# Row maxima that go to the shift row by DMA alone, tokens in another order, and new places in the plan

## The chip, the cores and the metric

The kernel runs on one core of a Trainium2 chip. Its time is that of one execution on the device, in microseconds (us); before and after are given as medians of several runs.

## The reference

Four transformer blocks run one after the other on x of shape (4, 512, 256), four batch entries of 512 tokens with 256 features; everything is float32. Each block has its own conditioning from `cond` (4, 256). Block 0 has one attention head over all 256 features; blocks 1 to 3 have 16 heads of 16 features. Cut to what the change touches, blocks 2 and 3 are:

```python
# block 2
h = layernorm(x, g1, be1) * (1 + scale_msa) + shift_msa
attn = softmax(einsum('blhd,bmhd->bhlm', q, k) * HD ** -0.5)      # q, k, v from h, 16 heads
x = x + gate_msa * (einsum('bhlm,bmhd->blhd', attn, v) @ Wproj + bproj)
x = x + gate_mlp * mlp(layernorm(x, g2, be2) * (1 + scale_mlp) + shift_mlp)
# block 3
att = softmax(einsum('bhqd,bhkd->bhqk', q, k)) / D ** 0.5
h1 = out_projection(att @ v) + x
x = h1 + sln(h1)
```

Block 1 normalises q and k to unit length (cosine attention) and has gates and an MLP like block 2. A softmax over the keys needs, for each query and head, something near the largest score to subtract before the exponential.

## The kernel before

**Jobs and layers.** The program works on 16 jobs, job j being layer j // 4 (the four blocks) for batch entry j % 4. Layers 1 to 3 are the many-headed ones (`multi(j)`); layer 1 is `bounded(j)`: there a cheap bound takes the place of the true maximum ("gmax", "shift1", "crow"). Layers 2 and 3 compute true maxima. A job's 16 heads are 4 units of 4 heads; units are numbered through, 4 j + g. All of this is unrolled, and nothing is looped on the chip.

**The plan.** `plan_steps` writes out one order of steps (kind, job or unit, index), from tables that give for each kind of step a time in ticks relative to its job: `QKV`, `ATTN`, `FFN`, `FFN3`, `OUTPUT`, `LAST`, `FOR_LAYER`, `FOR_LAST`, `SINGLE0` to `SINGLE3`, and so on. A job has 16 ticks (`TICKS`), 4 for a unit. Every engine walks through that one order and emits what it has to do for each step, so a place in a table sets the place in each engine's instruction stream. `PAIR`, `PAIR1`, `PAIR7` and `PAIR_LAST` say for every two ticks how scores, maxima, the products with V ("av") and the other steps ("0", "1") are mixed. `START` is the order of the first steps, given by hand.

**Attention of a unit.** SyncE stacks parts of q and k of the unit's heads into `SQ[u % 4]` and `SK[u % 4]` ("stack", six DMAs of 128 KB): rows 0 to 62 hold one head, rows 64 to 126 another, for two halves. Rows 63 and 127 of `SQ` are the shift row: minus the maximum of each query, which meets a 1 in `SK`, so the product that gives the scores already has the shift in it.

1. "max", 16 steps per unit, six ticks (`LEAD`) ahead of the unit's scores: a matmul (L657) of 128 queries (stationary, from `SQ`) against all 512 keys into a PSUM bank, and on VectorE a reduction (L1179) that writes minus the maximum of the 128 queries, one per partition, into a column of `m16`.
2. "shift", once per unit, four ticks after the unit's first maxima: TensorE waits for the last two maxima and transposes 80 columns of `m16` into a bank (L672); VectorE copies 16 rows of it into `cT` (L1186); SyncE waits for the copy and sends them with two DMAs (L554), 8 rows of 512 bytes each, to rows 63 and 127 of `SQ`.
3. "scores", 16 steps: a matmul (L680) of 128 keys against 512 queries, whose first waits for that transfer (`shifted`), and an exponential on ScalarE (L871) into one of 12 buffers `probs`.
4. "av": four matmuls (L693) on four column strips of the array, then a copy of the bank `AVB` to `oU`.

A maximum matmul takes rows 0 to 62 or 64 to 126, and the scores matmul beside it the other half, so the two run in pairs.

**Banks.** Everything but "av" uses seven PSUM banks in turn (`RING`): `claim` waits until the step seven uses earlier has been read out.

**Tokens.** "hT1" transposes the normalised input of a job from `tok1` (tokens on partitions, four tiles of 128) into a bank (L626) with token 128 t + p in column 128 t + p. At a job's end "oT1" transposes `oU` back (L718), from columns 128 i to 128 i + 127 to tile i. SyncE's queue is one queue for stacks, shift rows, weight loads, gates and stores, in the order of the plan.

The scratch of the step "headscale" (once, early) is in `m16`.

Of the kernel before, what the change touches and what calls it, by code (L numbers as in the profile page):

```python
# [13 lines left out]
P = 128  # L14
# [41 lines left out]
def direct(j):  # L56
# [5 lines left out]
SINGLE0 = {"stat1": (-16.0,), "norm1": (-19.05,), "hT1": (-15.0, -14.24), "q": (-9.06, -5.21), "k": (-5.7, -4.45),  # L62
           "v": (3.06, 6.72), "scores0": (-0.45, -0.1, 1.86, 3.41), "soft0": (1.86, 2.41, 4.61, 5.17),
           "pT0": (6.87, 7.42, 7.68, 8.53), "av0": (10.18, 10.73), "proj": (12.39, 13.94), "stat2": (13.99,),
           "norm2": (14.84,), "bias": (-2.75,)}
SINGLE1 = {"stat1": (-20.05,), "norm1": (-12.3,), "hT1": (-11.18, -11.13), "q": (-8.12, -4.91), "k": (-8.57, -5.36),
           "v": (3.1, 4.42), "scores0": (-1.64, -1.29, 1.78, 1.88), "soft0": (2.49, 2.84, 3.36, 3.71),
           "pT0": (7.11, 7.47, 7.82, 8.68), "av0": (11.73, 12.09), "proj": (13.16, 13.51), "stat2": (13.82,),
           "norm2": (14.33,), "bias": (-3.4,)}
SINGLE2 = {"stat1": (-17.0,), "norm1": (-16.55,), "hT1": (-9.6, -9.29), "q": (-6.76, -3.56), "k": (-5.65, -3.7),  # L70
           "v": (3.0, 4.07), "scores0": (-0.14, 0.81, 1.88, 2.23), "soft0": (2.59, 3.44, 3.96, 4.51),
           "pT0": (7.92, 8.38, 8.63, 8.99), "av0": (12.74, 12.9), "proj": (14.18, 14.28), "stat2": (16.29,),
           "norm2": (16.84,), "bias": (0.5,)}
FFN0 = {"hT2": (16.72, 17.27), "fc1": (20.62, 20.98, 21.33, 21.74, 24.73, 25.09, 26.87, 27.22), "gelu": (22.09, 27.58),
        "fc2a": (25.06, 25.81), "fc2": (30.32, 32.88)}
FFN2 = {"hT2": (24.65, 24.83), "fc1": (25.13, 25.31, 25.49, 25.67, 30.12, 30.29, 31.19, 31.87), "gelu": (26.05, 31.95),
        "fc2a": (28.47, 29.21), "fc2": (32.16, 32.27)}
FIRST = {("v", 0, 0): -4.01, ("v", 0, 1): -2.2, ("modrow", 0, 1): 1.96, ("headscale", 1, 0): -0.04, ("mod", 0, 1): 3.47,
# [3 lines left out]
NEXT1 = {("modrow", 1, 0): 16.25, ("mod", 1, 0): 22.0, ("load_mod", 1, 1): 24.0, ("modrow", 1, 1): 30.8,  # L82
         ("mod", 1, 1): 31.5, ("load_gate", 1, 0): 35.3, ("split_qkv", 1, 0): 45.87, ("load_qkv", 1, 1): 42.17,
         ("split_qkv", 1, 1): 49.41, ("load_qkv", 1, 2): 48.44, ("split_qkv", 1, 2): 49.75, ("load_qkv", 1, 0): 42.0,
         ("vones", 4, 0): 56.19, ("vones", 5, 0): 67.95}
LEAD_IN = {"stat1": (-25.59,), "norm1": (-23.73,), "hT1": (-14.74, -14.56), "qktok": (-12.53, -12.04, -11.51, -10.77),
           "qkss": (-12.22, -11.69, -11.15, -10.61), "qkroot": (-10.43,), "v": (-7.19, -6.91), "qkrs": (-10.19,),
# [3 lines left out]
           "shift1": (-0.98,), "crow": (-0.9, -0.22, 1.7, 1.7)}  # L91
# [118 lines left out]
def plan_steps():  # L210
# [4 lines left out]
    for w in range(BATCH, JOBS):  # L215
# [71 lines left out]
def cond_blocks_kernel(nc, x, cond, cols, rows, wqkv, wp, w1, w2, wmod, wgate, out):  # L287
# [3 lines left out]
    with ExitStack() as ctx:  # L291
# [1147 lines left out]
```

## Time and profile before

| | |
|---|---|
| median of 3 runs | 1176.04 us (1174.32 to 1178.96) |
| the profiled execution's own time | 1179.31 us |
| its span, first to last instruction | 1177.5 us |
| granted TensorE clock, mean | 0.98 |
| busy: TensorE, ScalarE, VectorE, GpSimdE | 94%, 69%, 60%, 42% |
| transfers on the hardware queue | 36288 packets, 63.20 MB, 20.1% of 16 engines' span |

The engines are PE (TensorE matmuls), PEld (its weight loads, which overlap them), DVE (VectorE), ACT (ScalarE), POOL (GpSimdE) and SP (SyncE, which issues the DMAs). "L672" is a line of the kernel's file. The busy time of an instruction includes its latency, and matmuls overlap, so the busy share of PE is above what the array is really in use. The name `m` in the rows is the tile `m16`, and `tok` stands for both `tok1` and `tok2`.

### The profile page before, as it was taken

The page shows a single profiled execution, that of the slowest core. Times are in us where ns is not written, and L with a number is a line of the kernel's source. Part 1 is how long each engine was busy: PE and PEld are TensorE (multiplying, and loading weights), DVE is VectorE, ACT ScalarE, POOL GpSimd, SP SyncE. Part 2 cuts the span into 40 slices and gives each one's busy share as a digit, 9 for nine tenths or more (in the row PEclk, how much of TensorE's full clock was granted, in tenths as well). Part 3 has the DMA queues.
Part 4 walks back from the last instruction along what each step waited for, and adds up shares of the span by engine and source line. Part 5 has one row for each costly group of instructions (what it writes and reads, how often), then busy time and mean ns, then how long its engine had stood idle before and what let it go on. Part 6 is the DMA issues. An engine that isn't in the chain of part 4 may idle for free.

```text
span 1177.5 us, 19700 instructions
## 1 busy us (share of the span) xinstructions
PE 1106.8 (94%) x6681; PEld 708.5 (60%) x6681; DVE 705.0 (60%) x1448; ACT 807.3 (69%) x1439; POOL 491.3 (42%) x447
## 2 busy tenths in 40 slices
PE   7799999889999999999999999999999999999985
PEld 5476877655665656657656566556566566545443
DVE  6463538535165364235864855865855756888884
ACT  2563655478788778796686776687686676676763
POOL 2452642523633635453345453354253345243232
PEclk8899999999999999999999989999999999999998
DMA  7010000223212203320122231132022202232201
GB/s 230 9 37 2 27 10 10 62 57 100 81 34 74 72 1 82 82 63 12 44 74 81 60 82 32 24 82 63 24 60 55 53 12 77 55 81 54 83 2 46
DMA packets 36386, 64.45 MB, mean 55 GB/s; under 512 B 7208, under 2 KB 22312, under 8 KB 36288
## 3 DMA queue, kind: packets, MB, share of 16 engines
q1 hardware_dynamic: 36288, 63.20, 20.1%
q8 instruction: 55, 0.90, 0.3%
q14 instruction: 43, 0.35, 0.1%
HBM read 22.90 MB, written 2.12 MB: 21 GB/s over the span
## 4 chain that ended last, share of the span: by engine, by line
PE 66%; DVE 11%; ACT 11%; issue 6%; POOL 3%; DMA 1%; SPq 0%; ACTq 0%; POOLq 0%; DVEq 0%
PE ring L583 12%; PE AVB L693 11%; PE ring L585 11%; PE ring L584 11%; PE ring L680 9%; PE ring L657 4%; DVE m L1179 4%; ACT probs L871 4%; PE ring L713 2%; ACT gT_h L937 2%; ACT L871 1%; DVE stats L1037 1%; POOL tok L1303 1%; PE ring L626 1%; ACT gT_f L937 1%
## 5 line engine op out<-in xcount | busy, mean ns | idle before, releaser
L871 ACT ACTIVATE probs<-ring 128x512 f32<-128x512 f32 x768 | 399.2, 618 | 126.0 <-PE ring L657 72.8
L1179 DVE TENSOR_REDUCE m<-ring 128x1 f32<-128x512 f32 x512 | 318.1, 682 | 111.2 <-PE ring L657 90.9
L680 PE MATMUL ring<-SQ,SK 64*128 64x512 f32 x768 | 237.4, 442 | 14.8 <-ACT probs L871 6.4
L657 PE MATMUL ring<-SK,SQ 63*128 63x512 f32 x512 | 198.7, 457 | 4.5 <-ACT probs L871 2.2
L680 PEld LDWEIGHTS ring<-SQ,SK 64*128 64x128 f32 x768 | 111.8, 187 | 146.8 <-issue 62.0
L693 PE MATMUL AVB<-probs,V 128*32 128x512 f32 x1536 | 191.5, 607 | 0.1
L1282 POOL TENSOR_TENSOR gT_l<-gT_f,gT_h 128x512 fp32r<-128x512 f32 x96 | 121.1, 1283 | 78.7 <-ACT gT_h L937 76.9
L583 PE MATMUL ring<-w_h,gT_h 128*128 128x256 f32 x384 | 110.2, 287 | 1.8 <-POOL gT_l L1282 1.8
L657 PEld LDWEIGHTS ring<-SK,SQ 63*128 63x128 f32 x512 | 85.6, 184 | 40.3 <-ACT probs L871 27.3
L584 PE MATMUL ring<-w_l,gT_h 128*128 128x256 f32 x384 | 107.0, 279 | 0.0
L585 PE MATMUL ring<-w_h,gT_l 128*128 128x256 f32 x384 | 106.9, 278 | 0.0
L1316 POOL TENSOR_TENSOR tmp<-tmp,gates 128x512 f32<-128x512 f32 x32 | 41.1, 1285 | 117.2 <-DVE tmp L1246 68.9
L693 PEld LDWEIGHTS AVB<-probs,V 128*32 128x32 f32 x1536 | 40.8, 109 | 81.5 <-issue 66.6
L937 ACT ACTIVATE gT_f<-ring,colv 128x512 f32<-128x512 f32 x96 | 66.9, 697 | 28.6 <-PE ring L585 26.0
L583 PE MATMUL ring<-postT_h,w_h 128*128 128x512 f32 x192 | 79.3, 413 | 3.8 <-ACT gT_h L937 1.9
L583 PEld LDWEIGHTS ring<-w_h,gT_h 128*128 128x128 f32 x384 | 72.6, 189 | 9.2 <-issue 3.3
L585 PE MATMUL ring<-postT_h,w_l 128*128 128x512 f32 x192 | 76.6, 399 | 0.0
L584 PE MATMUL ring<-postT_l,w_h 128*128 128x512 f32 x192 | 76.5, 398 | 0.0
L1277 POOL TENSOR_TENSOR hT_l<-hT_f,hT_h 128x512 fp32r<-128x512 f32 x30 | 38.5, 1287 | 90.2 <-ACT hT_h L811 90.1
L1246 DVE TENSOR_TENSOR tmp<-ring,rowp 128x512 f32<-128x512 f32 x40 | 27.6, 689 | 80.1 <-PE ring L585 80.0
L1277 POOL TENSOR_TENSOR postT_l<-postT_f,postT_h 128x512 fp32r<-128x512 f32 x24 | 31.3, 1305 | 101.9 <-ACT postT_h L811 101.6
L584 PEld LDWEIGHTS ring<-w_l,gT_h 128*128 128x128 f32 x384 | 72.5, 189 | 0.6
(183 smaller groups left out, 2163.9 us busy)
## 6 DMA issues: line engine op xcount, KB each, us to landing
SQ<-qh SPq DMA_DIRECT2D x96, 128.0 KB, 2.6
SK<-kh SPq DMA_DIRECT2D x96, 128.0 KB, 2.7
SQ<-ql SPq DMA_DIRECT2D x48, 128.0 KB, 2.6
SK<-kl SPq DMA_DIRECT2D x48, 128.0 KB, 2.8
raw<-in_w SPq DMA_DIRECT2D x20, 256.0 KB, 2.7
wmod_s<-in_wmod SPq DMA_DIRECT2D x6, 512.0 KB, 4.9
gates<-gate_rows SPq DMA_DIRECT2D x12, 256.0 KB, 3.8
raw<-in_wqkv SPq DMA_DIRECT2D x9, 256.0 KB, 2.8
```

Of the source, the lines that this page charges most:

```text
L583: pe.matmul(out, sh, mh, start=first, stop=False)
L584: pe.matmul(out, sh, ml, start=False, stop=False)
L585: return pe.matmul(out, sl, mh, start=False, stop=last)
L657: mm = pe.matmul(o[:, :], SQ[a % 4][r:r + KS, n // 2, c * P:(c + 1) * P], SK[a % 4][r:r + KS, n // 2, :], start=True, stop=True)
L680: mm = pe.matmul(o[:, :], SK[a % 4][r:r + KS + 1, n // 2, c * P:(c + 1) * P], SQ[a % 4][r:r + KS + 1, n // 2, :], start=True, stop=True)
L693: mm = pe.matmul(AVB[32 * n:32 * n + 32, :], V[j % 2][:, i, (HD + 1) * h:(HD + 1) * h + 32], probs[:, (4 * t + n) % PROBS, :], start=(i == ...
L871: act.activation(probs[:, n % PROBS, :], bank(kind, a, i)[:, :], ACT.Exp, scale=SCALE[layer(unit_job(a))]).then_inc(done["scores"], 1)
L937: ins = act.activation(dst[:, m % (MT // 2), :], bank("fc1", a, m)[:, :], ACT.Gelu, bias=colv[:, layer(a), col:col + 1])
L1179: nc.vector.tensor_reduce(m16[:, 80 * (a % 2) + col:80 * (a % 2) + col + 1], bank(kind, a, i)[:, :], AX_X, ALU.max, negate=True).then_inc( ...
L1277: nc.gpsimd.tensor_tensor(lo, full, hi.bitcast(F32), ALU.subtract).then_inc(done[kind], 1)
L1282: nc.gpsimd.tensor_tensor(gT_l[:, m, :], gT_f[:, m, :], gT_h[:, m, :].bitcast(F32), ALU.subtract).then_inc(g_lo, 1)
L1316: link(nc.gpsimd.tensor_tensor(y, y, g, ALU.mult))
```

## The change

- The step "shift" is gone from TensorE and VectorE. SyncE waits for the last two maxima and for the unit's stacks, and sends the maxima from `m16` itself with four DMAs, each 128 partitions by 4 floats (16 bytes per partition), into 512 consecutive floats of row 63 or 127 of one half of `SQ`.
- So that this gives the right order, position 4 p + t of a job of layers 1 to 3 now holds token 128 t + p. A helper `spread` picks every fourth column: where "hT1" writes the bank, where "max" reads its queries as stationary operand, and where "oT1" reads `oU`.
- "shift" no longer uses a bank of the ring, so the banks of all later steps change. VectorE's first two maxima of a unit now wait for the transfer of the unit two before, not for its transposition. `m16` becomes float32r, and "headscale" has its scratch in `rcp`.
- Most times in the tables, the patterns of pairs and the order of the first loads are new.

```diff
-QKV = {"hT1": (-19.2, -15.89), "q": (-12.95, -12.6), "k": (-12.75, -10.05), "v": (-8.75, -4.85),
-       "stack": (-8.25, -6.15, -1.05, 1.45), "stat1": (-22.45,), "norm1": (-21.15,)}
+QKV = {"hT1": (-19.2, -14.24), "q": (-12.95, -10.6), "k": (-12.7, -10.05), "v": (-8.75, -5.05),
+       "stack": (-8.25, -7.35, -2.05, 0.75), "stat1": (-22.15,), "norm1": (-21.3,)}
...
-PAIR_LAST = ("p8 A p6 0 p4 1", "p6 0 A p6 1", "p2 0 p6 1 A", "p4 0 a p6 1 b", "p6 A p8 0 p4 1", "A p6 0 p4 1", "p6 A p8 0 p4 1", "p4 0 p6 1 A")
+PAIR_LAST = ("p10 A p6 0 p2 1", "p4 A p8 0 p4 1", "p6 a p6 0 p2 b p2 1", "p4 0 a p4 1 b", "p6 A p8 0 p4 1", "A p4 0 p4 1", "p8 a p8 0 p2 b p2 1", "p4 0 p6 1 A")
...
-START = [("stat1", 0, 0), ("load_mod", 0, 0), ("load_qkv", 0, 1), ("load_qkv", 0, 0), ("load_qkv", 0, 2),
+START = [("stat1", 0, 0), ("load_mod", 0, 0), ("load_qkv", 0, 0), ("load_qkv", 0, 2), ("load_mod", 0, 1),
...
-RINGED = ("hT1", "v", "qktok", "q", "k", "max", "shift", "gmax", "shift1", "oT1", "oT2", "proj", "hT2", "fc1",
+RINGED = ("hT1", "v", "qktok", "q", "k", "max", "gmax", "shift1", "oT1", "oT2", "proj", "hT2", "fc1",
...
-        m16 = sb("m16", [P, 96])
+        m16 = sb("m16", [P, 96], F32R)
...
-            return 16 * 2 * ((u - UNITS * BATCH) // 4 + 1)
+            n = (u - UNITS * BATCH) // 4 + 1
+            return 16 * 2 * n if bounded(unit_job(u)) else 16 * (2 * UNITS + 4 * (n - UNITS))
...
                 elif kind == "shift":
 
-                    sp.wait_ge(done["shift"], nth("shift", a))
+                    sp.wait_ge(done["max"], max(nth("max", a, 14), nth("max", a, 15)))
+                    sp.wait_ge(stacked[a % 4], STACK_IN(a))
                     for par in range(2):
-                        d = SQ[a % 4][BLK * par + KS:BLK * par + KS + 1, :, :]
-                        dst = bass.AP(d.tensor, d.offset, [[2 * TOK, 1], [P, 8], [1, P]]).bitcast(F32)
-                        r = 32 * (a % 2) + 8 * par
-                        s = cT[r:r + 8, :]
-                        src = bass.AP(s.tensor, s.offset, [[P, 8], [P, 1], [1, P]]).bitcast(F32)
-                        sp.dma_start(dst, s.bitcast(F32)).then_inc(shifted[a % 4], 16)
+                        for half in range(2):
+                            m = 80 * (a % 2) + 8 * par + 4 * half
+                            sp.dma_start(SQ[a % 4][BLK * par + KS:BLK * par + KS + 1, half, :].bitcast(F32),
+                                         m16[:, m:m + 4].bitcast(F32)).then_inc(shifted[a % 4], 16)
...
+            def spread(x, t):
+
+                return x.rearrange("p (q t) -> p t q", t=TT)[:, t, :]
...
                     for t in range(TT):
-                        mm = pe.transpose(o[:, t * P:(t + 1) * P], src[:, t, i * P:(i + 1) * P], ident[:, :])
+                        to = spread(o, t) if kind == "hT1" and multi(a) else o[:, t * P:(t + 1) * P]
+                        mm = pe.transpose(to, src[:, t, i * P:(i + 1) * P], ident[:, :])
...
-                    mm = pe.matmul(o[:, :], SQ[a % 4][r:r + KS, n // 2, c * P:(c + 1) * P],
+                    mm = pe.matmul(o[:, :], spread(SQ[a % 4][r:r + KS, n // 2, :], c),
                                    SK[a % 4][r:r + KS, n // 2, :], start=True, stop=True)
...
-                elif kind == "shift":
-                    pe.wait_ge(done["max"], max(nth("max", a, 14), nth("max", a, 15)))
-                    mm = pe.transpose(o[0:80, 0:P], m16[:, 16 * (a % 2):16 * (a % 2) + 80], ident[:, :])
...
                     for g in range(UNITS):
-                        mm = pe.transpose(o[:, g * P:(g + 1) * P], oU[:, g, i * P:(i + 1) * P], ident[:, :])
+                        mm = pe.transpose(o[:, g * P:(g + 1) * P], spread(oU[:, g, :], i), ident[:, :])
...
                     if i < 2 and a - 2 >= UNITS * BATCH:
-                        dve.wait_ge(pe_ring, use("shift1", unit_job(a - 2)) if bounded(unit_job(a - 2)) else use("shift", a - 2))
+                        if bounded(unit_job(a - 2)):
+                            dve.wait_ge(pe_ring, use("shift1", unit_job(a - 2)))
+                        else:
+                            dve.wait_ge(shifted[(a - 2) % 4], SHIFT_IN(a - 2))
...
-                elif kind == "shift":
-                    dve.wait_ge(pe_ring, use(kind, a))
-                    for u in range(UNITS * (a // UNITS - 1), UNITS * (a // UNITS)) if bounded(unit_job(a - 2)) else (a - 2,):
-                        dve.wait_ge(shifted[u % 4], SHIFT_IN(u))
-                    r = 32 * (a % 2)
-                    nc.vector.tensor_copy(cT[r:r + 16, :], bank(kind, a)[64 * (a % 2):64 * (a % 2) + 16, 0:P]).then_inc(done["shift"], 1)
```

## Rows read from the trace of the kernel before

**Rows 1.** The head of the page: span, and busy time (share) and instructions by engine.
```profile
span 1177.5 us, 19700 instructions
PE 1106.8 (94%) x6681; PEld 708.5 (60%) x6681; DVE 705.0 (60%) x1448; ACT 807.3 (69%) x1439; POOL 491.3 (42%) x447
```

**Rows 2.** The chain of waits from 550 us on, its shares by line.
```profile
by line: PE AVB L693 13.9%; PE ring L680 11.8%; PE ring L583 11.4%; PE ring L584 10.0%; PE ring L585 9.9%; PE ring L657 7.6%; DVE m L1179 6.9%; issue 6.2%; ACT probs L871 4.0%; ACT L871 1.7%; DVE tok L1210 1.4%; PE ring L730 1.3%; DVE stats
```

**Rows 3.** Two windows: length, busy PE, PEld, DVE, ACT, POOL, clock, DMA.
```profile
550.00:850.00 300.00, 296.35 (x1847) 185.49 (x1843) 204.25 (x396) 216.30 (x384) 129.19 (x109) 0.99 0.22 56
850.00:1150.00 300.00, 288.26 (x1800) 168.81 (x1799) 220.48 (x431) 211.55 (x389) 115.40 (x118) 1.00 0.21 54
```

**Rows 4.** Groups by form: busy us, mean ns; idle before, and what ended it.
```profile
L672 PE MATMUL ring<-ident,m 128*80 128x128 f32 x32 | 9.7, 302 | 4.0 <-DVE m L1179 2.6 <-ACT hT_h L811 0.5
...
L1186 DVE CAST cT<-ring 16x128 fp32r<-16x128 f32 x32 | 8.9, 277 | 2.3 <-PE ring L672 1.8
...
L672 PEld LDWEIGHTS ring<-ident,m 128*80 128x80 f32 x32 | 3.7, 117 | 13.7 <-DVE m L1179 7.6 <-issue 3.5 <-DVE tok L1210 1.8
```

**Rows 5.** Timeline near 700 us: start, length, engine, instruction.
```profile
699.58 0.49 PE L657 MATMUL ring<-SK,SQ 63*128 63x512 f32 x1
...
700.00 0.31 PE L672 MATMUL ring<-ident,m 128*80 128x128 f32 x1
...
700.24 0.50 PE L680 MATMUL ring<-SQ,SK 64*128 64x512 f32 x1
```

**Rows 6.** Timeline of TensorE from 1038 us: scores matmuls that lead three pairs.
```profile
1038.28 0.50 PE L680 MATMUL ring<-SQ,SK 64*128 64x512 f32 x1
...
1038.62 0.40 PE L680 MATMUL ring<-SQ,SK 64*128 64x512 f32 x1
...
1038.85 0.39 PE L680 MATMUL ring<-SQ,SK 64*128 64x512 f32 x1
```

**Rows 7.** Timeline near 1056 us, in the last layer.
```profile
1056.00 0.50 PE L657 MATMUL ring<-SK,SQ 63*128 63x512 f32 x1
...
1056.63 0.31 PE L672 MATMUL ring<-ident,m 128*80 128x128 f32 x1
...
1056.77 1.11 PE L730 MATMUL ring<-ident,tok 128*128 128x128 f32 x8
```

**Rows 8.** Timeline of VectorE from 1087 us, and the chain of waits behind it.
```profile
1087.38 2.48 DVE L1179 TENSOR_REDUCE m<-ring 128x1 f32<-128x512 f32 x4
...
1093.21 0.67 SPq L554
...
1093.93 1.81 DMA SQ<-cT
```

**Rows 9.** Waits and issue times of SyncE's queue (ns: least, median, most).
```profile
SPq L554 <- DVE cT L1186: 408.5, 32, 33.1
...
L554 SPq DMA_DIRECT2D SQ<-cT x64: 623/655/1440, 555.0 to 1146.5; - x64
...
L462 SPq DMA_DIRECT2D condT<-in_cond x1: 453/453/453, 0.7 to 0.7; - x1
```

**Rows 10.** Chain of waits and timeline near 1102 us.
```profile
1101.86 0.69 DVE m L1179
...
1103.95 1.32 SPq L554 DMA_DIRECT2D SQ<-cT  x2
```

**Rows 11.** Timeline of the last unit, from 1143 us.
```profile
1143.03 0.68 DVE L1179 TENSOR_REDUCE m<-ring 128x1 f32<-128x512 f32 x1
...
1145.82 1.29 SPq L554 DMA_DIRECT2D SQ<-cT  x2
...
1148.40 0.80 PE L680 MATMUL ring<-SQ,SK 64*128 64x512 f32 x2 [1.97 <-ACT probs L871]
```

**Rows 12.** Timeline: weight loads of a job's output transpositions.
```profile
1052.94 1.73 PEld L718 LDWEIGHTS ring<-ident,oU 128*128 128x128 f32 x16 [0.24 <-ACT probs L871]
```

**Rows 13.** Waits of the weight path from 550 us on: us, times, longest.
```profile
PEld ring L657 <- ACT probs L871: 25.4, 79, 0.7
```

More of the change, by code:

```diff
@@ L58, in direct @@
     return layer(j) in (0, LAYERS - 1)
[L62 to L69, printed above, removed]
@@ new lines @@
+SINGLE1 = {"stat1": (-21.05,), "norm1": (-10.8,), "hT1": (-11.18, -10.83), "q": (-8.12, -4.31), "k": (-8.57, -7.36),
+           "v": (2.6, 3.92), "scores0": (-1.64, -1.29, 1.78, 1.88), "soft0": (2.49, 2.84, 3.36, 3.71),
+           "pT0": (7.11, 7.47, 7.82, 8.68), "av0": (11.73, 12.09), "proj": (13.16, 13.41), "stat2": (13.72,),
+           "norm2": (14.33,), "bias": (-5.4,)}
+SINGLE2 = {"stat1": (-17.0,), "norm1": (-16.55,), "hT1": (-9.6, -9.49), "q": (-6.76, -3.56), "k": (-5.65, -3.7),
+           "v": (3.0, 4.07), "scores0": (-0.14, 0.81, 1.78, 4.23), "soft0": (2.59, 3.44, 3.96, 4.51),
+           "pT0": (7.92, 8.38, 8.63, 8.99), "av0": (12.74, 12.9), "proj": (14.08, 14.48), "stat2": (16.29,),
+           "norm2": (16.94,), "bias": (0.2,)}
@@ new lines @@
+FFN0 = {"hT2": (16.72, 17.27), "fc1": (20.62, 20.98, 21.33, 21.74, 24.73, 25.09, 26.87, 27.22), "gelu": (22.09, 27.58),
+        "fc2a": (25.26, 25.96), "fc2": (30.57, 32.88)}
+FFN2 = {"hT2": (24.6, 24.78), "fc1": (25.13, 25.31, 25.49, 25.67, 30.02, 30.19, 31.09, 31.77), "gelu": (26.05, 31.85),
+        "fc2a": (28.17, 29.71), "fc2": (32.31, 32.57)}
+FIRST = {("v", 0, 0): -3.71, ("v", 0, 1): -2.1, ("modrow", 0, 1): 2.11, ("headscale", 1, 0): -1.34, ("mod", 0, 1): 3.47,
[3 rows of a table added]
+NEXT1 = {("modrow", 1, 0): 16.25, ("mod", 1, 0): 21.0, ("load_mod", 1, 1): 28.0, ("modrow", 1, 1): 30.8,
+         ("mod", 1, 1): 31.6, ("load_gate", 1, 0): 35.3, ("split_qkv", 1, 0): 45.87, ("load_qkv", 1, 1): 42.82,
+         ("split_qkv", 1, 1): 49.36, ("load_qkv", 1, 2): 46.14, ("split_qkv", 1, 2): 50.15, ("load_qkv", 1, 0): 42.0,
@@ new lines @@
+OUTPUT = {"gatefix": (20.35,), "final": (23.2, 24.35, 25.3, 28.0), "store": (27.2, 29.5, 29.75, 32.5), "bias": (19.1,)}
+LAST = {"bias": (-1.6,), "gatefix": (14.25,), "oT1": (16.15, 16.66, 17.17, 17.18), "oT2": (17.8, 18.11),
+        "proj": (18.95, 21.45), "base": (20.45, 25.75), "stat2": (22.5,), "centre": (23.35, 23.45, 23.55, 25.35),
+        "final": (24.65, 26.45, 28.2, 31.0), "store": (22.3, 23.75, 24.35, 24.45)}
+FOR_LAYER = {"gate": (7.7,), "gateout": (10.4,), "gatecast": (11.15, 28.25, 42.35, 56.45), "load_rows": (15.4,),
+             "load_mod": (11.95, 32.55), "modrow": (29.75, 46.4), "mod": (30.95, 47.05), "load_gate": (51.1,),
+             "load_qkv": (40.9, 43.2, 45.15), "split_qkv": (43.55, 45.3, 49.8), "load_wp": (7.0,), "split_wp": (8.4,),
+             "load_w1": (9.9, 11.9, 17.9, 19.35), "split_w1": (10.7, 12.7, 18.7, 20.8),
+             "load_w2": (13.9, 16.35, 22.15, 22.75), "split_w2": (14.7, 17.6, 23.55, 25.05)}
@@ new lines @@
+FOR_LAST = {"gate": (7.7,), "gateout": (11.35,), "gatecast": (15.25, 26.5, 45.15, 58.65), "load_rows": (15.1,),
+            "load_wp": (3.6,), "split_wp": (7.45,), "vones": (-14.55, 2.95)}
+PAIR = ("p6 A p6 0 p4 1", "p6 A p6 0 p4 1", "p8 A p2 0 p6 1", "p6 A p6 0 p4 1", "p6 A p8 0 p4 1", "p6 A p6 0 p6 1", "p6 A p6 0 p4 1", "p6 A p6 0 p4 1")
+PAIR_LAST = ("p10 A p6 0 p2 1", "p4 A p8 0 p4 1", "p6 a p6 0 p2 b p2 1", "p4 0 a p4 1 b", "p6 A p8 0 p4 1", "A p4 0 p4 1", "p8 a p8 0 p2 b p2 1", "p4 0 p6 1 A")
@@ L374, in bank @@
             return ring[USE[(kind, a, i)] % RING]
-        kinds = sorted({s[0] for s in PLAN if not s[0].startswith("load") and s[0] not in ("stack", "crow", "store", "gelu", "gateout", "gatecast", "gatefix")})
+        kinds = sorted({s[0] for s in PLAN if not s[0].startswith("load") and s[0] not in ("stack", "crow", "shift", "store", "gelu", "gateout", "gatecast", "gatefix")})
         done = {k: sem("done_" + k) for k in kinds}
@@ L954, in _ @@
                 nc.vector.memset(SK[i][:, :, :].bitcast(F32), 1.0)
-            nc.vector.memset(m16[:, :], 0.0)
+            nc.vector.memset(m16[:, :].bitcast(F32), 0.0)
             link(nc.vector.memset(mhalf[:, :], -0.5))
```

69 lines of the change are left out of this document (25 added, 44 removed), and 10 rows, old and new, of tables (FIRST, START).

## Prediction

> **What bounds the kernel now.** I read the head of the page first [rows 1]: the span is 1177.5 us, TensorE shows work in 94% of it, VectorE in 60%. A matmul's duration includes its way through the array, so 94% is not an array at its peak; what a removed instruction gives back has to be read between the starts of its neighbours. The change touches the maxima, and those exist in the stretch from 550 us on alone, so I then read the chain of waits there [rows 2]: nearly all of the listed shares are TensorE lines, the largest VectorE line is the maximum reduction (L1179, 6.9%), "issue" has 6.2%. The two halves of that stretch differ little for TensorE [rows 3], 296.35 of 300 us and 288.26 of 300 us; VectorE goes from 204.25 to 220.48 us. So the first half (the third layer's units) is TensorE's, and in the second half VectorE sets the pace here and there.
>
> **What goes: the transposition on TensorE.** There are 32, one per unit of four heads. Their weight loads are busy 3.7 us and stand behind 13.7 us of idle weight path, mostly a wait for the last maximum [rows 4]. Two places show the price between neighbours. In the third layer the matmul before starts at 699.58, the transposition at 700.00, the next pair at 700.24 [rows 5]: 0.66 us, where two neighbouring pairs are 0.34 us apart (1038.28 to 1038.62) and in a tight run 0.23 us (1038.62 to 1038.85) [rows 6]. That is 0.32 us each over the 0.34. In the last layer the same three starts are 1056.00, 1056.63 and 1056.77 [rows 7]: 0.77 us, so 0.43 us each. Lower bound: the array time alone, 3.7 us in all. Upper bound: the load and the idle ahead of it, 3.7 + 13.7 = 17.4 us. I take 16 x 0.32 = 5.1 us for the third layer, where TensorE is the bound. In the last layer 16 x 0.43 = 6.9 us would be the whole of it, but there VectorE paces part of the units.
>
> **What goes: the copy on VectorE.** 32 copies of 277 ns, 8.9 us [rows 4]; they stand between maximum reductions. In the third layer they are covered by VectorE's slack of 95 us [rows 3] and worth nothing. In the last layer 16 x 0.277 = 4.4 us is what a unit gains where VectorE paces it. For the last layer's 16 units I take the middle of 4.4 and 6.9, 5.7 us. Also gone: 32 uses of a ring bank, each held from the transposition to the copy. The next user of that bank comes seven uses on, so I cost this at nothing beyond the above.
>
> **What moves: from the last maximum to the shift row.** Now it is reduction, transposition, copy, two DMAs, landing. SyncE waited 408.5 us in 32 waits for the copy [rows 9], so this step ends whatever the queue does before it. One issue takes 655 ns in the median (most 1440) [rows 9]; the second landed 1.81 us after its start [rows 8]. New: the queue waits for the maxima themselves and issues four. With 0.67 us from start to start the fourth starts 2.0 us after the last maximum and lands 2.0 + 1.8 = 3.8 us after it. Nearest row for a transfer in 16-byte pieces: the load of condT, 256 pieces, issue 453 ns [rows 9]; with 0.5 us an issue it would be 3.3 us. I take 3.8. Before: where the transposition follows at once (reduction ends 1101.86 + 0.69 = 1102.55, issues from 1103.95 [rows 10]) it is 1.4 + 0.7 + 1.8 = 3.9 us, the same as the new 3.8. Where the transposition stands later it is longer: maxima done at 1087.38 + 2.48 = 1089.86, row complete at 1093.93 + 1.81 = 1095.74, so 5.9 us [rows 8]. So this path is nowhere longer at that price, and it is up to 2.1 us shorter where the chain runs through it (1093.21 to 1095.74). The last unit shows the wait plainly: its reduction ends at 1143.03 + 0.68 = 1143.71, the row's DMAs start at 1145.82, and its scores start at 1148.40 after 1.97 us of idle TensorE, which the view puts down to ScalarE [rows 11]; with 3.8 us they start near 1147.55, 0.85 us earlier. With two or three such places in the last layer I take 2.5 us, bounds 0 and 6. Two extra issues per unit are 32 x 1.34 = 43 us on SyncE, which has 408.5 us of waiting at this very step; behind them stand the next unit's six stack transfers and the gate casts, and they now leave earlier or at the same time, since the queue is released one transposition and one copy sooner. The new wait of VectorE (the first two maxima of a unit wait for the transfer of the unit two before) costs nothing: that unit's scores waited for the same transfer and start two ticks earlier. SyncE's added wait for the stacked operands is met, since the maxima read them.
>
> **What is added: access with a step of four elements.** The third and fourth layers' 512 maximum matmuls load their weights from every fourth column, and so do 192 of the output transpositions (L718, 12 jobs); 96 input transpositions (L626) write their bank with that step. The trace has no such load. At step one, loads in a row start 0.11 us apart (16 in 1.73 us, from 1052.94 [rows 12]), and the transpositions run at the pace of the loads. Lower bound: the same, 0. Upper bound: twice as long, so +0.11 us for each of 704. Why not all of it counts: in the tight run the load is hidden behind the other pair (0.23 us [rows 6]), in the other pairs it is exposed (0.34 us). With two thirds of the third layer's 256 exposed, 18 us; in the last layer half of that, 9 us, as VectorE paces; and all 192 transpositions, 21 us: 48 us. I take 0, by the row it is nearest to: the moving operand comes in at 0.23 us for 512 columns, 0.45 ns each, the load at 0.11 us for 128, 0.86 ns each, so a load has about twice the time for an element that this memory is seen to need. For the strided write the transposition has 0.05 us of array time in 0.11, so twice as slow stays hidden: 0.
>
> The Trainium skill, "SBUF — State Buffer", section "Door 1: The DMA port swizzle", speaks against this: a line of SBUF has 16 bytes and at least two accesses have to fall into one line for full speed, and this step gives one each; by it the sum would be worse by the 48 us above. "PSUM — Partial Sum Buffer", "Specifications (TRN2)", says that any non-contiguous pattern slows matmuls, which would touch the 96 input transpositions. No row here shows either.
>
> **What is moved: places.** Almost every time in the tables moves by a tenth to a few ticks (a tick is about 600 us / 128 = 4.7 us), the first loads and the patterns of pairs change. No row prices this; the waits that places steer are those of TensorE's weight path for ScalarE and VectorE. I take 0 and bound it by 7 us either way, about a quarter of the largest of those waits that ends with another engine, 25.4 us [rows 13].
>
> **Sum.** 5.1 + 5.7 + 2.5 = 13.3 us less. The profiled execution took 1179.31 us with its span of 1177.5; it becomes 1166.0. The median of the runs, 1176.04, lies 3.3 us below that execution, so I forecast 1162.7, rounded 1163 us.
>
> **Rivals.**
> 1. Strided loads are slower (ends on the other side). Place: the 512 + 192 loads. For: the loads stand exposed in the 0.34 us pairs and set the pace of the transpositions. Against: the load is the slower of TensorE's two readers. Price 48 us, time 1163 + 48 = 1211. It decides from 13.3 / 704 = 19 ns per load if all are exposed, 30 ns with the shares above.
> 2. The transfer in 512 pieces is the new wait. If an issue takes the longest seen, 1.44 us [rows 9], the row is complete 4.3 + 1.8 = 6.1 us after the last maximum, where the last unit now needs 4.7 (1143.71 to 1148.40) [rows 11]. At 2.2 us for some six tight units of the last layer, 13 us, it eats the gain: 1176. For: four issues in a row. Against: the 453 ns of the nearest row.
> 3. The saving is only VectorE's in the last layer and half of TensorE's in the third, since the waits reappear at the next bank: 4.4 + 2.6 = 7 us, 1169. For: 13.7 us of idle stood ahead of the loads [rows 4] and something else may keep it. Against: 0.24 of the 0.66 us at 700 us is the transposition's own start to the next [rows 5], which no wait can keep.
> 4. The places move it, 7 us beyond the sum either way: 1156 or 1170. For and against: nothing but their number.
>
> **How the numbers follow.** Forecast 0.50, at 1163, its own range 1155 to 1170. Saving halved (3) 0.14. New wait (2) 0.12. Strided loads (1) 0.16. Places (4) 0.08, at 1156 or 1170 and beyond. I leave out most of the strided case (0.13) and 0.05 at the low end: range 1152 to 1185. A measurement here tells about 0.5% (5.9 us) from no change. In the order forecast, (3), (2), (1), (4): faster, below 1170.2, 0.47 + 0.09 + 0.03 + 0.02 + 0.04 = 0.65; within, 0.02 + 0.04 + 0.04 + 0.01 + 0.02 = 0.13; slower, above 1182, 0.01 + 0.01 + 0.05 + 0.13 + 0.02 = 0.22.
>
> **What would show it.** Right: no TensorE row from the maxima tile but the four of the second layer; the weight loads of the maximum matmuls still 0.18 us and pairs 0.34 and 0.23 us apart; output transpositions 0.11 us apart; the row complete some 3.3 to 4 us after the last maximum; few waits of scores for the maxima's transfer; VectorE busy 8.9 us less. Wrong: loads of 0.29 us and pairs 0.44 us apart (1); issues over 1 us, and scores waiting for the transfer at each unit of the last layer (2); idle time ahead of the weight loads grown by what the transpositions had (3).

## The result, and the profile after

| | before | after |
|---|---|---|
| median | 1174.49 us (1172.51 to 1178.96, 6 runs) | 1182.56 us (1181.27 to 1185.45, 6 runs) |
| ratio after / before | | 1.0069, 95% interval 1.0054 to 1.0084 |
| span of the profiled execution | 1177.5 us | 1179.5 us |

The change made the kernel 8.1 us slower, 0.7%; 1163 us and "faster" were forecast. The two profiled executions differ by 2 us only (1179.31 and 1181.27 us): that of before took longer than any of its six timed runs, that of after was the shortest of its own. So sizes come from the medians here, and the traces say where they arise.

The head of the page of the kernel after, against [rows 1]:

```profile
span 1179.5 us, 19634 instructions
PE 1117.2 (95%) x6649; PEld 745.7 (63%) x6649; DVE 696.7 (59%) x1416; ACT 807.3 (68%) x1439; POOL 491.8 (42%) x447
```

TensorE has 32 matmuls less and 10.4 us more of busy time, and its weight loads 37.2 us more. VectorE lost the 32 copies and 8.3 us. The same two windows as in [rows 3]:

```profile
550.00:850.00 300.00, 298.66 (x1820) 203.15 (x1822) 197.81 (x377) 215.29 (x382) 131.35 (x111) 1.00 0.22 54
850.00:1150.00 300.00, 295.46 (x1800) 188.61 (x1794) 219.77 (x418) 213.19 (x392) 115.33 (x118) 1.00 0.23 53
```

In the last layer TensorE went from 288.26 to 295.46 of 300 us: that layer is now TensorE's as well. The chain of waits from 550 us on says the same [rows 2]: the maximum matmuls (now L662) grew from 7.6% to 13.9%, and the maximum reduction (L1184) is no longer among the large shares:

```profile
by line: PE ring L682 17.9%; PE AVB L695 17.6%; PE ring L662 13.9%; PE ring L587 11.8%; PE ring L589 10.0%; PE ring L588 9.9%; PE ring L720 2.8%; issue 1.8%; PE ring L631 1.6%; ACT gT_h L939 1.5%; ACT probs L873 1.3%; PE ring L732 1.3%; DVE
```

What changed in these instructions stands in the views of one line each (durations in ns: least, median, most). First the maximum matmuls and their loads in the kernel before, then in the one after, where the output transpositions (L720) and the input transpositions (L631) follow:

```profile
L657 PEld LDWEIGHTS ring<-SK,SQ x512: 182/183/188, 524.6 to 1141.8; 63*128 63x128 f32 x171
L657 PE MATMUL ring<-SK,SQ x512: 386/492/506, 524.6 to 1141.8; 63*128 63x512 f32 x171
```

```profile
L662 PEld LDWEIGHTS ring<-SK,SQ x512: 304/306/314, 523.4 to 1143.8; 63*128 63x128 f32 x171
L662 PE MATMUL ring<-SK,SQ x512: 386/616/811, 523.4 to 1143.8; 63*128 63x512 f32 x171
L720 PEld LDWEIGHTS ring<-ident,oU x192: 195/209/221, 321.0 to 1164.3; 128*128 128x128 f32 x192
L631 PEld LDWEIGHTS ring<-ident,tok x224: 137/141/230, 11.7 to 1057.1; 128*128 128x128 f32 x112
```

By the medians a load takes 123 ns longer. The shortest of the 512 is 304 ns, where the longest of before was 188, so it is no contention that comes and goes. The output transpositions' loads went from 141 to 209 ns. The input transpositions, which write with the same step, have the durations of before. The timeline of TensorE shows where the longer load stands (start, length), first in the kernel before, then after, with one of the loads:

```profile
698.94 0.40 PE L680 MATMUL ring<-SQ,SK 64*128 64x512 f32 x1
699.09 0.49 PE L657 MATMUL ring<-SK,SQ 63*128 63x512 f32 x1
699.42 0.39 PE L680 MATMUL ring<-SQ,SK 64*128 64x512 f32 x1
```

```profile
702.12 0.40 PE L682 MATMUL ring<-SQ,SK 64*128 64x512 f32 x1
702.15 0.62 PE L662 MATMUL ring<-SK,SQ 63*128 63x512 f32 x1
702.61 0.40 PE L682 MATMUL ring<-SQ,SK 64*128 64x512 f32 x1
```

```profile
702.14 0.30 PEld L662 LDWEIGHTS ring<-SK,SQ 63*128 63x128 f32 x1
```

From the maximum matmul to the scores matmul behind it there are 0.46 us instead of 0.33. Over all places of the third layer where scores, maximum and scores follow each other directly (69 before, 46 after, worked out from the records), that median went from 336 to 458 ns: the matmul behind a maximum starts later by the whole 122 ns. But this is not yet time lost. From scores to scores it is 0.48 us here before and 0.49 after, because the maximum matmul now starts 0.03 us behind the scores instead of 0.15. How much of the load is in the time shows only beside a kernel with the same plan and short loads, which is e1.

The transfers did as forecast. SyncE's issues (ns), its wait for the maxima from 550 us on (us, times, longest), and the timeline of the last unit's row (first VectorE, then SyncE, then TensorE), against [rows 9, 11]:

```profile
L553 SPq DMA_DIRECT2D SQ<-m x128: 469/601/1787, 544.4 to 1147.6; - x128
```

```profile
SPq L553 <- DVE m L1184: 213.7, 26, 19.1
```

```profile
1142.70 3.08 DVE L1184 TENSOR_REDUCE m<-ring 128x1 fp32r<-128x512 f32 x5 [0.73 <-PE ring L662]
1145.82 2.40 SPq L553 DMA_DIRECT2D SQ<-m  x4
1149.74 2.17 PE L682 MATMUL ring<-SQ,SK 64*128 64x512 f32 x8 [1.80 <-DMA SQ<-m]
```

From the last maximum (1145.78) to the scores there are 3.96 us; before there were 4.7. It is the only place where the view of waits has TensorE waiting for this transfer (1.8 us, once).

### The profile page after: what moved, and what is told of

It reads as the page before. It is cut to its first block, busy times and chain, and to the rows that moved or that the text cites. A ratio compares the mean times of both kernels' runs of the same rounds, so it can differ in the third digit from the quotient of the medians.

```text
span 1179.5 us, 19634 instructions
## 1 busy us (share of the span) xinstructions
PE 1117.2 (95%) x6649; PEld 745.7 (63%) x6649; DVE 696.7 (59%) x1416; ACT 807.3 (68%) x1439; POOL 491.8 (42%) x447
## 4 chain that ended last, share of the span: by engine, by line
PE 73%; ACT 10%; DVE 8%; POOL 4%; issue 4%; DMA 1%; SPq 0%; POOLq 0%; ACTq 0%; DVEq 0%
PE AVB L695 13%; PE ring L587 12%; PE ring L682 12%; PE ring L588 10%; PE ring L589 10%; PE ring L662 8%; ACT probs L873 2%; ACT gT_h L939 2%; PE ring L720 2%; PE ring L631 2%; ACT gT_f L939 2%; PE ring L715 1%; POOL gT_l L1281 1%; DVE m L1165 1%; DVE stats L1039 1%
## 5 line engine op out<-in xcount | busy, mean ns | idle before, releaser
L1184 DVE TENSOR_REDUCE m<-ring 128x1 fp32r<-128x512 f32 x512 | 319.5, 682 | 126.7 <-PE ring L662 126.2
L682 PE MATMUL ring<-SQ,SK 64*128 64x512 f32 x768 | 245.6, 440 | 11.8 <-ACT probs L873 3.5
L662 PE MATMUL ring<-SK,SQ 63*128 63x512 f32 x512 | 221.3, 530 | 3.5 <-ACT probs L873 2.0
L682 PEld LDWEIGHTS ring<-SQ,SK 64*128 64x128 f32 x768 | 116.2, 190 | 140.5 <-issue 63.3
L695 PE MATMUL AVB<-probs,V 128*32 128x512 f32 x1536 | 194.7, 615 | 0.0
L662 PEld LDWEIGHTS ring<-SK,SQ 63*128 63x128 f32 x512 | 131.9, 306 | 29.2 <-ACT probs L873 18.5
L587 PEld LDWEIGHTS ring<-w_h,gT_h 128*128 128x128 f32 x384 | 72.2, 188 | 13.3 <-issue 6.5
L589 PEld LDWEIGHTS ring<-w_h,gT_l 128*128 128x128 f32 x384 | 72.5, 189 | 0.0
```

The source lines that it names most:

```text
L587: pe.matmul(out, sh, mh, start=first, stop=False)
L589: return pe.matmul(out, sl, mh, start=False, stop=last)
L662: mm = pe.matmul(o[:, :], spread(SQ[a % 4][r:r + KS, n // 2, :], c), SK[a % 4][r:r + KS, n // 2, :], start=True, stop=True)
L682: mm = pe.matmul(o[:, :], SK[a % 4][r:r + KS + 1, n // 2, c * P:(c + 1) * P], SQ[a % 4][r:r + KS + 1, n // 2, :], start=True, stop=True)
L695: mm = pe.matmul(AVB[32 * n:32 * n + 32, :], V[j % 2][:, i, (HD + 1) * h:(HD + 1) * h + 32], probs[:, (4 * t + n) % PROBS, :], start=(i == ...
L1184: nc.vector.tensor_reduce(m16[:, 80 * (a % 2) + col:80 * (a % 2) + col + 1], bank(kind, a, i)[:, :], AX_X, ALU.max, negate=True).then_inc( ...
```

## The experiments

Each was timed beside the kernel before on the same chip. The median of the kernel before was 1174.33 us beside e1 to e4, 1174.79 beside e5 to e8 and 1173.96 beside e9 and e10, so ratios to it are given too, with their 95% intervals.

### e1_plainmax

```diff
-                    mm = pe.matmul(o[:, :], spread(SQ[a % 4][r:r + KS, n // 2, :], c),
+                    mm = pe.matmul(o[:, :], SQ[a % 4][r:r + KS, n // 2, c * P:(c + 1) * P],
```

> The changed kernel with one edit: the 512 maximum matmuls load their weights from 128 neighbouring columns again instead of every fourth. The maxima then belong to other queries than the shift row has them, so the result is another; the amount of work is the same. Theory A (the strided loads ate the gain): a load is back at 0.18 us from 0.31, the pairs are closer together, and the time falls by some 21 us, the 13 forecast and the 8 lost, to 1155 to 1167. Theory B (the new places or the shifted banks are to blame): the time stays at 1178 to 1184 although the loads are short. Theory C (the four transfers of small pieces hold the scores): stays above 1176, with scores that wait for the transfer.

1167.14 us, ratio 0.9934 (0.9918 to 0.995). This is the changed kernel with contiguous loads in its maximum matmuls and nothing else different: 15.4 us less than with the step. Theory A has the direction right; the time is at the upper edge of its 1155 to 1167, because 21 us were expected and 15.4 came. The group of the loads, at 185 ns:

```profile
L662 PEld LDWEIGHTS ring<-SK,SQ 63*128 63x128 f32 x512 | 85.5, 185 | 40.6 <-ACT probs L873 32.2 <-ACT gT_h L939 2.8 <-ACT postT_h L813 1.9
```

From the first scores of the third layer to the first of the last layer the two traces take 341.2 (changed) and 333.8 us (e1), from there to the last unit's first scores 245.1 and 239.7: 7.4 and 5.4 us, so both layers pay.

The two kernels have the same order of instructions on TensorE, so their starts can be compared place by place (timeline of e1, then of the changed kernel at the same instructions):

```profile
733.77 0.50 PE L682 MATMUL ring<-SQ,SK 64*128 64x512 f32 x1
733.77 0.73 PE L662 MATMUL ring<-SK,SQ 63*128 63x512 f32 x2
734.11 0.62 PE L682 MATMUL ring<-SQ,SK 64*128 64x512 f32 x2
```

```profile
738.67 0.50 PE L682 MATMUL ring<-SQ,SK 64*128 64x512 f32 x1
738.67 0.72 PE L662 MATMUL ring<-SK,SQ 63*128 63x512 f32 x2
739.13 0.50 PE L682 MATMUL ring<-SQ,SK 64*128 64x512 f32 x2
```

Here the step from scores to scores grew from 0.34 to 0.46 us. Worked out from the records of both layers, for scores, maximum and scores in a row:

- 51 places that were under 0.30 us apart went to 0.36 in the median, and 20 places at 0.30 to 0.35 to 0.46. Both show the whole load.
- 25 places at 0.45 to 0.50 us stayed at 0.49. They show nothing of it.
- Where two maximum matmuls follow each other (113 places), their starts are 0.33 us apart in both kernels, so a load of 306 ns fits in between.

In sum, 50 of the third layer's 64 groups of four scores matmuls grew by about 120 ns, the difference of one load, though some four maximum matmuls go with each. Together these groups became 6.0 us longer, of the layer's 7.4.

### e2_step2

```diff
-                return x.rearrange("p (q t) -> p t q", t=TT)[:, t, :]
+                return x.rearrange("p (h q t) -> p h t q", h=2, t=2)[:, t // 2, t % 2, :]
...
-                            sp.dma_start(SQ[a % 4][BLK * par + KS:BLK * par + KS + 1, half, :].bitcast(F32),
-                                         m16[:, m:m + 4].bitcast(F32)).then_inc(shifted[a % 4], 16)
+                            for pair in range(2):
+                                sp.dma_start(SQ[a % 4][BLK * par + KS:BLK * par + KS + 1, half, 2 * P * pair:2 * P * (pair + 1)].bitcast(F32),
+                                             m16[:, m + 2 * pair:m + 2 * pair + 2].bitcast(F32)).then_inc(shifted[a % 4], 16)
```

> The changed kernel with the tokens in yet another order, so that each strided access has a step of two elements, not four; the shift row then takes eight transfers of 8-byte pieces per unit. The result is the reference's. Theory A with a memory line of four elements of which two must be used: the load is at 0.18 to 0.19 us, and the time falls to 1160 to 1170, less what the eight issues (4.9 us instead of 2.4) cost the tight units of the last layer, some 1 to 2 us at each of six. Theory A with a cost for any step: loads of 0.31 us and 1182 to 1190. Theory B: 1180 to 1186 whatever the load takes. Theory C: clearly slower than the changed kernel, since there are twice as many pieces and issues.

1182.27 us, ratio 1.0065 (1.005 to 1.0081): no better than the change. The 1160 to 1170 us of theory A, with the few microseconds that it allowed for the issues, did not come, and the time alone would fit theory B. But the loads are nearly as short as contiguous ones:

```profile
L663 PEld LDWEIGHTS ring<-SK,SQ x512: 189/192/335, 521.0 to 1142.0; 63*128 63x128 f32 x171
```

So the step of two makes the loads short again, but the time does not fall. What stands in their place is eight issues in a row, which e5 tests. In units 24 to 32 the eighth issue starts 4.4 to 5.7 us after the last maximum (worked out from the records), where the fourth and last of e1 starts after 1.8 to 2.4, and the view of waits of the last layer shows who waits for it:

```profile
PE ring L683 <- DMA SQ<-m: 13.0, 5, 4.3
```

Those 13 us are the size by which e2 lies above e1 (15.1). The output transpositions' loads stayed at 208 ns with the step of two.

### e3_oldplaces and e4_newplaces

e3 is the changed kernel with all tables, patterns and `START` of the kernel before; e4 is the kernel before with those of the changed one.

> The changed kernel's transfers, strides and waits with every table of places, the patterns of pairs and the order of the first loads as before. The result is the reference's. Theory A: the loads cost as in the changed kernel, so 1180 to 1190, no faster than the changed kernel. Theory B: the new places are the loss, so this is at 1160 to 1172. Theory C: 1180 to 1190.

> The kernel before with the new tables of places, patterns of pairs and order of the first loads, and nothing else of the change. The result is the reference's. Theory A: places are worth little, 1170 to 1180. Theory B: the places alone lose 8 us or more, 1182 to 1190.

e3: 1180.08 us, ratio 1.0046 (1.0031 to 1.0061), loads at 306 ns. e4: 1172.37 us, ratio 0.9982 (0.9968 to 0.9997). The places alone win 2 us in the kernel before; in the changed one they seem to lose 2.5 (1180.08 to 1182.56), but there the intervals overlap. They are neither the loss nor a gain worth the name, as theory A has it for both.

### e5_early

e2 with its eight transfers in two groups of four: the first, for the maxima of the first two query tiles, two ticks earlier.

```diff
-            shift = [("shift", u - 1, 0)] if v % TT == 0 and u - 1 < UNITS * JOBS and not bounded((u - 1) // UNITS) else []
+            shift = [("shift", u - 1, 1)] if v % TT == 0 and u - 1 < UNITS * JOBS and not bounded((u - 1) // UNITS) else []
+            if v % TT == 2 and u < UNITS * JOBS and not bounded(u // UNITS):
+                shift = [("shift", u, 0)]
...
-                    sp.wait_ge(done["max"], max(nth("max", a, 14), nth("max", a, 15)))
+                    sp.wait_ge(done["max"], max(nth("max", a, 8 * i + 4 + n) for n in range(4)))
```

> The kernel with a step of two (e2_step2), whose eight transfers per unit now go in two groups: four after the second quarter of the unit's maxima, two ticks earlier, and four after the last. The result is the reference's. Theory A2 (a step of two costs the load nothing, and e2_step2 lost its 15 us against e1_plainmax to eight issues in a row ahead of the last layer's scores): the chain behind the last maximum is as short as with four transfers, so 1165 to 1171. Rival (the number of pieces, or of issues on the queue, is what costs, wherever they stand): 1177 to 1185.

1174.46 us, ratio 0.9995 (0.9984 to 1.0006): 7.8 us less than e2 for the order of the issues alone, with loads at 193 ns. So where the issues stand costs, against the rival; but the 1165 to 1171 us of theory A2 were not reached either. The waits for the transfer went from 13.0 us to:

```profile
PE ring L685 <- DMA SQ<-m: 5.2, 4, 1.8
```

### e6_early_act

e5, and ScalarE's copy of `AVB` to `oU` puts the columns in tile order, so that the output transpositions load contiguously.

```diff
-                        mm = pe.transpose(o[:, g * P:(g + 1) * P], spread(oU[:, g, :], i), ident[:, :])
+                        mm = pe.transpose(o[:, g * P:(g + 1) * P], oU[:, g, i * P:(i + 1) * P], ident[:, :])
...
-                    act.activation(oU[:, g, :], AVB[:, :], ACT.Copy).then_inc(unit_out, 1)
+                    act.activation(oU[:, g, :].rearrange("p (h t q) -> p h t q", h=2, t=2),
+                                   AVB[:, :].rearrange("p (h q t) -> p h t q", h=2, t=2), ACT.Copy).then_inc(unit_out, 1)
```

> e5_early with the output transpositions reading neighbouring columns again: ScalarE puts the columns in order when it copies the bank AVB to oU, reading and writing with steps. The result is the reference's. If the strided loads of the 192 output transpositions are what they look like in the changed kernel's trace (120 ns from start to start instead of 109), TensorE gains 192 x 0.011 = 2 us; if ScalarE's 48 copies stay at 0.61 us, the time is 1 to 2 us below e5_early; if they get slower by 0.2 us or more each, it is the same or above.

1172.22 us, ratio 0.9976 (0.9965 to 0.9987), 2.2 us less than e5, as expected, though the two intervals just touch. The reordering copy is as long as the plain one (609 ns, 610 in e5), and the transpositions' loads are back at 141 ns:

```profile
L912 ACT ACTIVATE oU<-AVB 128x512 f32<-128x512 f32 x48 | 29.2, 609 | 21.4 <-PE AVB L698 21.0
L723 PEld LDWEIGHTS ring<-ident,oU 128*128 128x128 f32 x192 | 21.0, 141 | 6.1 <-issue 6.1
```

So the step in the output transpositions is worth some 2 us, in size the same as 192 x 11 ns, by which their starts moved apart (from 109 to 120 ns, worked out from the records). What was left against e1 shows in the wait for the second group (view of waits, then timeline). The longest is at 1098.48 us; there SyncE had been stacking and storing when the maxima were ready (1090.97, worked out from the records), and the second group left at 1094.47 only:

```profile
PE ring L685 <- DMA SQ<-m: 6.3, 3, 3.2
```

```profile
1098.48 0.47 PE L685 MATMUL ring<-SQ,SK 64*128 64x512 f32 x1 [3.18 <-DMA SQ<-m]
...
1090.93 0.59 SPq L539 DMA_DIRECT2D SQ<-ql  x1
1091.57 0.60 SPq L539 DMA_DIRECT2D SQ<-qh  x1
1092.21 1.52 SPq L539 DMA_DIRECT2D SK<-kh  x2
1093.77 0.60 SPq L539 DMA_DIRECT2D SK<-kl  x1
1094.47 5.06 SPq L556 DMA_DIRECT2D SQ<-m  x8
```

### e7_oldct

e1 with the kernel before's two transfers from `cT` (8 rows of 512 bytes) at the same place and on the same wait for the maxima, but neither transposition nor copy. The shift rows hold what `cT` holds, not this unit's maxima.

> e1_plainmax with the two transfers of cT of the kernel before in place of the four of m16, released by the last maxima all the same. The shift rows of the last two layers then hold what cT held last, so the result is another; transposition and copy are gone. This is the whole saving with the old transfers. Theory D (what was missing of the forecast saving is eaten by four issues and small pieces): 1158 to 1163, clearly below e1_plainmax at 1167. Theory E (the saving was over-estimated: TensorE's waits reappear elsewhere): 1165 to 1168, as e1_plainmax.

1167.66 us, ratio 0.9941 (0.9924 to 0.9958), the same as e1: theory E, the saving was over-estimated. Four issues in 16-byte pieces instead of two in rows of 512 bytes cost nothing that can be measured in the time. In the trace they do cost a little at the last unit: its scores start 2.61 us after the last maximum (worked out from the records) where e1 has 3.96, but the stretch from there to the end is 31.4 us instead of 30.1.

### e8_spread_io

The kernel before with the new order of tokens alone: input transpositions write with step four, output transpositions read with step four; transposition, copy and contiguous maximum loads stay.

> The kernel before with the tokens in the changed order and nothing else: the 96 input transpositions write their bank with a step of four, the 192 output transpositions load every fourth column, the maxima load neighbouring columns. The result is the reference's. Theory A with these as part of it: 192 x 0.011 = 2 us from the loads and nothing from the writes, so 1175 to 1178. If the strided writes cost too: 96 x 0.1 = 10 us, 1184 to 1188.

1175.66 us, ratio 1.0004 (0.9991 to 1.0017), in the range of theory A. Both steps together cost at most 2 us. Input transpositions' loads 145 ns, as in the kernel before.

### e10_before_strided_loads

The kernel before with one edit, the step in the maximum matmuls' loads.

```diff
-                    mm = pe.matmul(o[:, :], SQ[a % 4][r:r + KS, n // 2, c * P:(c + 1) * P],
+                    mm = pe.matmul(o[:, :], spread(SQ[a % 4][r:r + KS, n // 2, :], c),
```

> The kernel before with one edit: the stationary operand of a maximum matmul is read with step four (every fourth query of the unit) instead of contiguously; the row maxima then belong to other queries. Nothing else changes. Theory A (a load with step four takes 306 ns instead of 184 and cannot hide under the 435 ns of a pair): loads of about 0.306 us, and the time 13 to 18 us longer, 1187 to 1192, ratio 1.011 to 1.016, as the changed kernel against its twin with contiguous loads (15.4 us). Theory B (the loads cost so much only together with the four transfers or the changed places of the new kernel): loads still 0.306, time within 5 us of the kernel before, ratio under 1.004.

1188.53 us, ratio 1.0121 (1.0101 to 1.0141), as theory A has it: 14.6 us for this one edit, in the other kernel, with transposition, copy, two transfers and old places.

```profile
L661 PEld LDWEIGHTS ring<-SK,SQ 63*128 63x128 f32 x512 | 134.1, 307 | 29.1 <-ACT probs L875 14.4 <-DVE tok L1214 3.5 <-DVE m L1183 2.6
```

### e9_stack_later

e6 with three kinds of issues put behind the second group.

```diff
-       "stack": (-8.25, -7.35, -2.05, 0.75), "stat1": (-22.15,), "norm1": (-21.3,)}
+       "stack": (-8.25, -7.35, -1.9, 0.75), "stat1": (-22.15,), "norm1": (-21.3,)}
...
-OUTPUT = {"gatefix": (20.35,), "final": (23.2, 24.35, 25.3, 28.0), "store": (27.2, 29.5, 29.75, 32.5), "bias": (19.1,)}
+OUTPUT = {"gatefix": (20.35,), "final": (23.2, 24.35, 25.3, 28.0), "store": (27.2, 30.1, 30.2, 32.5), "bias": (19.1,)}
```

> e6 with three kinds of transfer moved on SyncE's queue: in the layers of row maxima one stacking step (third time of "stack") goes from -2.05 to -1.9, and two output stores from 29.5 and 29.75 to 30.1 and 30.2, so that they are issued behind the second group of maxima transfers instead of ahead of it. Theory A (what is left of e6 against e1 is SyncE being busy with stacking and stores when the maxima of units 24 and 28 are ready: gaps of 1.75 and 3.56 us before their scores, where e1 has 0.24): the second group starts within 1 us of the last maximum in those units, the gaps fall to some 0.3 us, and the time is 4 to 5 us under e6's 1172.2: 1166 to 1169, ratio to the kernel before 0.993 to 0.995. Theory B (the gaps are only where a slack shows that is spent elsewhere): no change, 1171 to 1173. Theory C (the stacked blocks come later and their own maxima wait): maxima of units 26 and 30 wait on the stacking, 1173 or more.

1170.43 us, ratio 0.9972 (0.9956 to 0.9989). The wait fell as theory A has it, from 6.3 us in 3 places to:

```profile
PE ring L685 <- DMA SQ<-m: 1.7, 1, 1.7
```

The time did not follow to the 1166 to 1169 us expected: 1.8 us less than e6, and the two intervals overlap. In the trace the units up to the 29th of 32 start as in e1 (1094.94 and 1094.56 us), and 1.4 us are lost between there and the last unit. Of these 1.1 us fall between 1102.4 and 1104.2 us, behind a job's output transpositions: there the chain of waits goes through VectorE's reading of their bank (L1212, L1213) before the next maximum matmul, where in e1 it stays on TensorE. What holds VectorE up there was not tested. Of the versions that leave out nothing it is the shortest here, 3.5 us under the kernel before and 12 under the changed one; e1 at 1167 us, with its shorter loads, suggests that up to 3 more are there.

## Why the prediction was wrong

**The step that failed** is the price of the strided loads: "I take 0, by the row it is nearest to", reasoned from 0.45 ns for an element of the moving operand against 0.86 for one of the load. A load with step four takes 306 ns and not 183, and it costs 15.4 us in the changed kernel (e1) and 14.6 in the kernel before (e10). That is more than the whole forecast gain. The row that the estimate went by compares two different readers, at step one both; it says nothing of what a reader pays for a step.

The measured 1182.56 us lies inside the range of 1152 to 1185 all the same, because that range was stretched for a piece of the strided case; a slower kernel had been given a chance of 0.22.

The prediction named this as rival 1, and the signs it gave for it (loads of 0.29 us, pairs 0.44 us apart) are what the trace shows, at 0.31 and 0.46. Its price, 48 us, was nearly three times too high (15.4 + 2). The 512 loads became 63 us longer in sum; a quarter of that is in the time, 30 ns per load. The prediction had two thirds exposed in one layer and a third in the other, at 0.11 us: 18 and 9 us, where e1 shows 7.4 and 5.4. Its picture of where the load hides was wrong too. It took the tight run (0.23 us) to hide it and the 0.34 us pairs to show it; both show it whole (0.36 and 0.46 us in the changed kernel). What swallows the rest is the pairs that already stood 0.49 us apart, pairs of maximum matmuls, and idle weight path, which shrank from 40.6 us ahead of these loads in e1 to 29.2 here:

```profile
L662 PEld LDWEIGHTS ring<-SK,SQ 63*128 63x128 f32 x512 | 131.9, 306 | 29.2 <-ACT probs L873 18.5 <-ACT gT_h L939 2.7 <-ACT postT_h L813 1.9
```

The output transpositions, priced at 21 us in that rival, cost 2 (e6 against e5): their loads grew by 68 ns, their starts, 120 ns apart, moved by 11 only, so these loads overlap.

The Trainium skill, "SBUF — State Buffer", section "Door 1: The DMA port swizzle", was quoted and then overruled: a line of 16 bytes wants two or more accesses for full speed. For the maximum loads the measurement agrees with it on both sides: one element per line 306 ns, two per line (e2) 192, four 183. It does not fit the output transpositions, whose loads take 208 ns with two elements per line as with one. The two kinds of load differ in more than their step: 63 rows against 128, and `SQ` is declared float32r where `oU` is float32; no run varied either. The Trainium skill's remark in "PSUM — Partial Sum Buffer", "Specifications (TRN2)", that any non-contiguous pattern slows matmuls significantly, did not show in the input transpositions' writes: 273 ns for the matmul with and without the step.

**The saving was real, and half of what was forecast.** e1 is the mechanism with contiguous maximum loads: 5.2 us under e4, the kernel before at the same places; with the 2 us of the output transpositions set aside, some 7 us for transposition, copy and a shorter chain, where 13.3 were forecast. No run takes these three apart. The windows of e4 and of e1, each from the first scores of the third layer to those of the last layer, and from there to the last unit, say where:

```profile
560.90:897.30 336.40, 332.14 (x2079) 210.81 (x2078) 225.73 (x438) 247.63 (x437) 147.13 (x124) 1.00 0.22 56
897.30:1140.30 243.00, 236.64 (x1482) 133.22 (x1481) 192.96 (x378) 172.16 (x322) 92.75 (x99) 0.99 0.22 53
```

```profile
562.20:896.00 333.80, 329.35 (x2061) 209.91 (x2060) 221.69 (x422) 247.51 (x437) 146.93 (x124) 1.00 0.23 56
896.00:1135.80 239.80, 233.98 (x1467) 131.38 (x1466) 189.02 (x363) 172.30 (x321) 92.75 (x99) 0.99 0.23 54
```

- Third layer: forecast 5.1 us, found 2.6 (336.4 to 333.8), after the longer starts of its 64 output transpositions have taken back 0.7. With those set aside it is 0.21 us for each transposition, not 0.32. That is near rival 3's "half", but waits did not come back (idle TensorE 4.3 and 4.5 us): the 0.32 was read at one place, and the mean over 16 is smaller. (The lower bound given there as "the array time alone, 3.7 us" is the busy time of the transpositions' loads [rows 4]; nothing hangs on it.)
- Last layer up to the last unit: forecast 5.7 and 2.5 together, found 3.2. VectorE lost 3.9 us of work, and idle TensorE went from 6.4 to 5.8 us only. The chain that got shorter seldom set the time: by the views of waits TensorE waited in e4 twice for the row (2.0 us) and once for a maximum ahead of the transposition (2.0 us), and e1 still has 1.7 us for the row and 1.2 for maxima.

**What held.** Issues at 0.6 us each, the row complete some 4 us after the last maximum, 3.96 from there to the scores where 3.8 was said, and no unit but the last waiting for it: rival 2 was rightly put aside, and e7 shows that pieces and number of transfers cost nothing measurable. Something like it came true only where eight issues stood in a row (e2); that its 13 us of waiting are the very figure of the rival is chance, since the rival had slow issues in mind and these take 601 ns. Strided writes at 0 held, as far as e8 can tell (both steps together at most 2 us). Places within 7 us held: 2 us (e4).

**The sum as measured.** Places -2.1 (e4), mechanism with contiguous loads -5.2 (e1 against e4), step of the maximum loads +15.4 (after against e1): +8.1 us. Each term is the step from one kernel to the next, so they add up to the measured difference by construction, and that is no check of them. The check is e10, which has 14.6 for the last term in another kernel. Each may be off by 1 to 2 us, and the term of the places depends on the kernel in which it is taken (e3).

## What to carry to other kernels

A transfer that does away with a transposition sends its bill through the layout: look first at who must now read with a stride, and multiply by how often. Here 32 transpositions were traded for 512 loads. Where no row shows an access pattern and a known rule names a penalty, 0 is not the neutral value, and a ratio between two other readers is no substitute. Nor would the full bound have done: with its 48 us the forecast would have been 1211, 28 us too high. One edit to the kernel before (e10) prices the pattern without any of the change. An order in pieces of two elements can be had for twice the transfers, and pays only where the queue that issues them is given room: the same eight transfers cost 8 us more in one block than in two halves.

## What the runs showed of the hardware

- A weight load of 63 rows by 128 columns of four bytes (float32r) took 183 ns contiguous, 192 at step two, 306 at step four. One of 128 by 128 float32 for a transposition took 141 ns contiguous and 208 at step two and at step four. Why the second behaves otherwise is open.
- Of a load that became 123 ns longer, all showed where two scores matmuls with a maximum between them had stood 0.24 or 0.34 us apart, and nothing where they had stood 0.49 us apart or where two maximum matmuls followed each other at 0.33 us.
- In a row of transpositions a load longer by 67 ns moved the starts apart by 11 ns.
- ScalarE's copy from a bank to SBUF took 609 ns with its columns reordered in steps of two, 605 to 610 without.
- A transfer of 128 pieces of 16 bytes held SyncE's queue for 601 ns in the median, one of 8 rows of 512 bytes for 655.
